# Power attention of a decoder: scores from single-pass products of split queries and keys, two heads at once

## What is computed

```python
q = (x @ Wq).reshape(B, T, 16, 128)          # 16 query heads
k = (x @ Wk).reshape(B, T, 8, 128)           # 8 key heads, each used by 2 query heads
v = (x @ Wv).reshape(B, T, 8, 128)
logG = cumsum(log_sigmoid(6.906768 + x @ Wg))
qk = einsum('bthd,bshd->bhts', q, k) / sqrt(128)
a  = where(causal, qk ** 2 * exp(logG[t] - logG[s]), 0)
y  = einsum('bhts,bshd->bthd', a, v) / (sum(a) + 1e-6)
out = y @ Wc + bc                            # then x + out and a layer norm
```

## Time and profile before

| what | value |
|---|---|
| median of 3 runs | 2582.27 us (2581.72 to 2593.28) |
| the profiled execution, its own time | 2584.34 us |
| its span, first to last instruction | 2582.6 us |
| TensorE busy | 2235.2 us, 87% of the span |
| VectorE, ScalarE, GpSimd busy | 1204.0, 981.8, 679.0 us |
| mean granted TensorE clock | 0.916 of full speed |
| chain that ended last, by engine | PE 22%, issue 6%, DVE 6%, ACT 4% |
| matmul line 330, high weights by high x | 384 matmuls of 512 columns, 397 ns each |

### The profile page before, as it was taken

The page is one execution under the profiler, slowest core; times in us unless marked ns, Lnnn a source line. Parts: engine busy times, 40 slices in busy tenths (PEclk is TensorE's granted clock), DMA queues, the critical chain, the costliest instruction groups (busy, mean ns, idle before and its releaser), DMA issues. The chain is left out here.

```text
span 2582.6 us, 38373 instructions
## 1 busy us (share of the span) xinstructions
PE 2235.2 (87%) x14368; PEld 1799.7 (70%) x14368; DVE 1204.0 (47%) x3113; ACT 981.8 (38%) x2234; POOL 679.0 (26%) x693
## 2 busy tenths in 40 slices
PE   5999999999998688878999999858898847888774
PEld 3989988988987466666888877656565436767542
DVE  2343333343335566655111113336777745677656
ACT  2222222222222466633121111223655635777632
POOL 2442332332231121112343410023443331332110
PEclk8999999999999767789999999887999868999886
DMA  5000000000000110010010000023332130000001
GB/s 191 1 29 13 9 29 13 9 21 13 9 1 1 64 44 26 1 54 33 25 50 17 17 1 1 1 49 53 51 54 49 28 114 13 14 26 10 1 9 65
DMA packets 34631, 78.08 MB, mean 30 GB/s; under 512 B 5264, under 2 KB 17680, under 8 KB 31504
## 3 DMA queue, kind: packets, MB, share of 16 engines
q1 hardware_dynamic: 34448, 75.63, 10.4%
HBM read 55.16 MB, written 4.19 MB: 23 GB/s over the span
## 5 line engine op out<-in xcount | busy, mean ns | idle before, releaser
L1108 PE MATMUL PS<-WH,bXH 128*128 128x512 f32 x512 | 200.9, 392 | 5.4 <-POOL WL L1385 5.4
L1108 PE MATMUL PS<-WL,bXH 128*128 128x512 f32 x512 | 200.4, 391 | 0.0
L1108 PE MATMUL PS<-WH,bXL 128*128 128x512 f32 x512 | 200.4, 391 | 0.0
L558 DVE TENSOR_TENSOR xN<-PS,xN 128x512 f32<-128x512 f32 x128 | 88.5, 691 | 228.0 <-PE PS L361 228.0
L1790 DVE TENSOR_REDUCE aM<-PS 128x4 f32<-128x1024 f32 x128 | 155.0, 1221 | 52.1 <-PE PS L1630 51.1
L1303 DVE SCALAR_TENSOR_TENSOR s<-s,cf,PS 128x256 f32<-128x256 f32 x112 | 53.8, 480 | 249.1 <-ACT s L1223 240.1
L1733 ACT ACTIVATE aPT<-PS 128x1024 f32<-128x1024 f32 x128 | 129.4, 1024 | 69.8 <-PE PS L1650 68.5
L1223 ACT ACTIVATE s<-PS 128x256 f32<-128x256 f32 x128 | 49.0, 383 | 277.3 <-PE PS L1108 277.3
L330 PE MATMUL PS<-aXH,QKH 128*128 128x512 f32 x384 | 152.3, 397 | 0.0
L643 POOL TENSOR_TENSOR E<-E,DM 128x256 f32<-128x256 f32 x64 | 47.1, 736 | 392.4 <-ACT E L475 392.4
L330 PE MATMUL PS<-aXH,QKL 128*128 128x512 f32 x384 | 149.6, 390 | 0.0
(11 more groups left out here) (405 smaller groups left out, 6264.1 us busy)
## 6 DMA issues: line engine op xcount, KB each, us to landing
sg<-in_gu SPq DMA_DIRECT2D x8, 1024.0 KB, 4.9
aqs<-aQH SPq DMA_DIRECT2D x64, 128.0 KB, 4.2
gQK<-in_Wqk SPq DMA_DIRECT2D x8, 768.0 KB, 4.2
V<-in_xT SPq DMA_DIRECT2D x4, 1024.0 KB, 6.3
gC<-in_Wc SPq DMA_DIRECT2D x8, 512.0 KB, 3.6
xN<-in_x SPq DMA_DIRECT2D x4, 1024.0 KB, 8.7
cst<-in_cT SPq DMA_DIRECT2D x8, 512.0 KB, 4.8
cV<-in_c SPq DMA_DIRECT2D x8, 512.0 KB, 4.0
```

The source lines that it names most:

```text
L558: e.tensor_tensor(xN[:, t, :], PS[:, b, :], xN[:, t, :], ALU.add).then_inc(o_add.sem, 1)
L1108: mm = e.matmul(PS[:, b, :], x[:, kc, 128 * t:128 * t + 128], w[:, kc, :], start=kc == 0 and i == 0, stop=kc == KC - 1 and i == 2)
```

## The change

The projected queries and keys are stored as two F32R tiles, `qkH` and `qkL`, in place of the float32 tile `qk`. ScalarE writes `qkH` for all three m (three copies a step instead of two); VectorE writes `qkL` as the difference of PSUM and `qkH` (three subtractions a step instead of one copy), and releases the PSUM room. The scores of both heads of a sequence are one product: three single-pass matmuls of 512 columns (2 heads by 256 queries, first 128 keys) into the first bank, and three of 256 columns (2 heads by 128 queries, last 128 keys) into the first half of the second bank. The square reads the 768 columns in one run; `sq` and `aT` have the new order of columns; the multiply into `aT` becomes two instructions, of 512 and 256 columns; the logits' copy before turn 0 becomes one instruction in place of two.

```diff
-        qk = W("qk", [128, 3, 512])
+        qkH, qkL = W("qkH", [128, 3, 512], F32R), W("qkL", [128, 3, 512], F32R)
...
-        sq = W("sq", [128, 2, 384])
-        aT = W("aT", [128, 2, 2, 384])
+        sq = W("sq", [128, 768])
+        aT = W("aT", [128, 2, 768])
...
-    qk_mm, q_out, k_out = K.flag("pe_qk", 3 * N), K.flag("act_q", 2 * N), K.flag("dve_q", N)
+    qk_mm, q_hi, q_lo = K.flag("pe_qk", 3 * N), K.flag("act_q_hi", 3 * N), K.flag("dve_q_lo", 3 * N)
...
             for m in range(3):
-                R.use(("qk", n, m), 1, k_out.upto(n + 1) if m == 1 else q_out.upto(2 * n + 1 + m // 2))
+                R.use(("qk", n, m), 1, q_lo.upto(3 * n + m + 1))
...
                 for h in (0, 1):
-                    e.matmul(PS[:, b, 130 * h:130 * h + 129], aT[:, j, h, 0:128], v0, start=True, stop=True,
+                    e.matmul(PS[:, b, 130 * h:130 * h + 129], aT[:, j, 256 * h:256 * h + 128], v0, start=True, stop=True,
                              skip_group_check=True)
...
                 if j == 0:
-                    e.wait_ge(*q_out.upto(2 * n + 2))
-                    e.wait_ge(*k_out.upto(n + 1))
-                for h in (0, 1):
-                    q0 = 256 * j
-                    e.matmul(PS[:, b + h, 0:256], qk[:, 2, q0:q0 + 128], qk[:, h, q0:q0 + 256], start=True, stop=True)
-                    mm = e.matmul(PS[:, b + h, 256:384], qk[:, 2, q0 + 128:q0 + 256], qk[:, h, q0 + 128:q0 + 256],
-                                  start=True, stop=True, skip_group_check=True)
+                    e.wait_ge(*q_hi.upto(3 * n + 3))
+                    e.wait_ge(*q_lo.upto(3 * n + 3))
+                q0 = 256 * j
+                for i, (k, q) in enumerate(pair3((qkH, qkH), (qkL, qkL))):
+                    e.matmul(PS[:, b, :], k[:, 2, q0:q0 + 128], q[:, 0:2, q0:q0 + 256], start=i == 0, stop=i == 2)
+                for i, (k, q) in enumerate(pair3((qkH, qkH), (qkL, qkL))):
+                    mm = e.matmul(PS[:, b + 1, 0:256], k[:, 2, q0 + 128:q0 + 256], q[:, 0:2, q0 + 128:q0 + 256],
+                                  start=i == 0, stop=i == 2)
                 mm.then_inc(s_mm.sem, 1)
...
-            for m in (0, 2):
+            for m in range(3):
                 b = rooms["qk", n, m][0]
                 if m == 0 and n:
                     e.wait_ge(*s_mm.upto(2 * n))
                 e.wait_ge(*qk_mm.upto(3 * n + m + 1))
-                e.activation(qk[:, m, :], PS[:, b, :], ACTF.Copy).then_inc(q_out.sem, 1)
+                e.activation(qkH[:, m, :], PS[:, b, :], ACTF.Copy).then_inc(q_hi.sem, 1)
...
-                    e.activation(sq[:, :, :], PS[:, b:b + 2, 0:384], ACTF.Square, scale=SC).then_inc(s_sq.sem, 1)
+                    e.activation(sq[:, :], PS[:, b:b + 2, :].rearrange("p a c -> p (a c)")[:, 0:768], ACTF.Square, scale=SC).then_inc(s_sq.sem, 1)
...
-            e.tensor_copy(aT[0:8, p % 2, 0, :], PS[0:8, b, 0:384])
-            e.tensor_copy(aT[0:8, p % 2, 1, 0:128], PS[0:8, b, 384:512]).then_inc(lg_out.sem, 1)
+            e.tensor_copy(aT[0:8, p % 2, 0:512], PS[0:8, b, :]).then_inc(lg_out.sem, 1)
...
                 if n:
                     e.wait_ge(*s_mm.upto(2 * n))
-                e.wait_ge(*qk_mm.upto(3 * n + 2))
-                e.tensor_copy(qk[:, 1, :], PS[:, rooms["qk", n, 1][0], :]).then_inc(k_out.sem, 1)
+                for m in range(3):
+                    e.wait_ge(*q_hi.upto(3 * n + m + 1))
+                    e.tensor_tensor(qkL[:, m, :], PS[:, rooms["qk", n, m][0], :], qkH[:, m, :].bitcast(F32),
+                                    ALU.subtract).then_inc(q_lo.sem, 1)
...
-                    e.tensor_tensor(aT[:, j, :, :], sq[:, :, :], E[:, j:j + 1, :].broadcast_to([128, 2, 384]),
-                                    ALU.mult).then_inc(s_at.sem, 1)
+                    for c, w, k in ((0, 512, 0), (512, 256, 256)):
+                        at = e.tensor_tensor(aT[:, j, c:c + w].rearrange("p (h q) -> p h q", h=2),
+                                             sq[:, c:c + w].rearrange("p (h q) -> p h q", h=2),
+                                             E[:, j:j + 1, k:k + w // 2].broadcast_to([128, 2, w // 2]), ALU.mult)
+                    at.then_inc(s_at.sem, 1)
```

More of the change, by code:

```diff
@@ L314, in tensor @@
             for i in range(4):
-                src = aT[0:8, p % 2, 0, 128 * i:128 * i + 128] if i < 3 else aT[0:8, p % 2, 1, 0:128]
+                src = aT[0:8, p % 2, 128 * i:128 * i + 128]
                 mm = e.transpose(PS[:, b, 32 * p + 8 * i:32 * p + 8 * i + 8], src, idF[0:8, 0:8])
@@ L377, in attend @@
                 for h in (0, 1):
-                    e.matmul(PS[:, b, 130 * h:130 * h + 129], aT[:, j, h, 0:128], v0, start=True, stop=True,
+                    e.matmul(PS[:, b, 130 * h:130 * h + 129], aT[:, j, 256 * h:256 * h + 128], v0, start=True, stop=True,
                              skip_group_check=True)
                 for h in (0, 1):
-                    e.matmul(PS[:, b + 1, 130 * h:130 * h + 129], aT[:, j, h, 128:256], v0, start=True, stop=False,
+                    e.matmul(PS[:, b + 1, 130 * h:130 * h + 129], aT[:, j, 256 * h + 128:256 * h + 256], v0, start=True, stop=False,
                              skip_group_check=True)
-                    mm = e.matmul(PS[:, b + 1, 130 * h:130 * h + 129], aT[:, j, h, 256:384], v1, start=False,
+                    mm = e.matmul(PS[:, b + 1, 130 * h:130 * h + 129], aT[:, j, 512 + 128 * h:640 + 128 * h], v1, start=False,
                                   stop=True, skip_group_check=True)
```

## The result

The changed kernel takes 2568.42 us (median of 14 runs, 2562.87 to 2579.85), the kernel before 2587.76 us (14 runs, 2576.10 to 2598.24; the 2582.27 us shown above were the median of the first three of them). The ratio is 0.9932 with a 95% interval of 0.9913 to 0.9951: 0.7% faster, some 18 us. The profiled execution of the changed kernel took 2577.13 us, with a span of 2575.4 us; it is one of its slower ones.

A forecast was written before the change was run, and what follows sets the result against it. TensorE's queue was taken to bound layer 0's self attention. Scores -16.2, split multiply +0.2 and logits copies -0.2 sum to -16.2 us, giving 2566 us against the median of 2582.27; range 2557 to 2576.

The forecast's parts named there:

- TensorE's queue is the time in turns 0 to 29: Layer 0's self attention: TensorE always busy, so one microsecond out of its queue is one microsecond of the kernel.
- 2.62 against 2.08 us: TensorE's time for one turn's scores, before and after the change; a gain of 0.54 us a turn.
- the upper bound: 512-column scores at 0.230 us: 0.007 us extra for each of 12 matmuls, 0.08 us a turn, 2.5 us in all.
- 30 turns count: Of 32 turns with scores, all but turns 30 and 31 give 0.54 us each, 16.2 us together.
- there the shorter scores only lengthen that wait: Turns 30 and 31: TensorE already waits 1.84 and 1.83 us for `yN`, so shorter scores gain nothing there.
- the 0.2 us forecast for the start: Before turn 0, four times two logits copies become one: -0.2 us in all, between 0 and -1.1.
- ScalarE and VectorE cost nothing: Each turn: ScalarE's extra 0.60 us copy and VectorE's three 0.68 us subtractions fit in idle time.
- 1.8: Microseconds to spare between VectorE's last subtraction of a turn and its first add of `out`.
- The split multiply: Multiply into `aT` as two instructions: 0.08 us for each j, hidden in normal turns, +0.2 us in turn 31.
- The gain is made and partly lost later: Rival: after 786 us low-clock stretches may shift; gain sinks to 8 us, 2574 us; chance 0.22.
- Weight loads that don't hide: Rival: 12 score weight loads a turn in the open, 1.3 us more a turn, 2605 us; chance 0.04.
- VectorE late at the transposes: Rival: VectorE over 0.9 us later at `attended`, TensorE waits, gain gone, 2582 us; chance 0.04.

The follow-up runs named there:

- fill_norm_turns: Changed kernel plus 8 overwritten TensorE matmuls in `turn`, meant ahead of the yN waits of turns 30 and 31; 2583.37 us, ratio 0.9953 to the kernel before.
- two and four products: Changed kernel without the low-keys-by-high-queries score product: 2546.1 us, ratio 0.9840; with low keys by low queries added: 2588.22 us, 1.0009 (to the kernel before).
- fill_scores: Changed kernel plus 8 overwritten TensorE matmuls ahead of the second sequence's score products in turns 30 and 31; 2578.73 us, ratio 0.9946 to the kernel before.

## Why the prediction was right

Forecast were 2566 us and 16.2 us of gain; measured were 2568.42 us, a ratio of 0.9932, and on three chips or sets of runs 0.9932, 0.9946 and 0.9916. That is the side and about the size. The nearness of the whole is partly luck. The self attention gave 13.7 us and not 16.2. The stages after cross0 gave 3.4 us that nobody forecast: from the first product with the experts' weights on, both profiles of the kernel before take 1453.1 and 1453.2 us, and eleven of the twelve profiles of the changed kernel and its variants 1449.3 to 1450.0 (`fill_norm_turns` has 1453.2). It lies in the attention stages of the second layer, whose code is the same; the cause is open. And the kernel before, from whose first three runs the 2566 us were counted, has a median 5.5 us higher over all 14. Step by step:

- **TensorE's queue is the time in turns 0 to 29**: shown. No wait of TensorE came up in normal turns, and the queue's slope is one to one between two and four products.
- **2.62 against 2.08 us**: the old side was right, the new one is 2.11, since the 512-column products come at 0.233 and not at 0.2267 us. I had named this pace as the upper bound, but tied it to the two runs of columns; with one run it is the same. The isolated-stream figure of the Trainium skill ("TensorE: Matmul & The Clock Gate", "Back-to-back issue gap") is 0.216 us for 512 columns. The trace does not agree: 0.227 to 0.233, each with a weight load of its own.
- **30 turns count**: right for the scores, since the waits of turns 30 and 31 grew from 1.84 to 2.36 us. But "there the shorter scores only lengthen that wait" was the step that failed: the longer wait let the clock fall, which cost 1.6 us. `fill_scores` takes the wait away and the 1.6 us come back. So 14.1 us reach the end of the stage in place of 16.2: 30 x 0.51 = 15.3 from the turns, 0.4 from the start, less 1.6 for the clock. The 0.4 is chance: the first score matmul starts at 80.1 us where it was 80.5, but at 79.2 and 81.9 in the other two profiles of the changed kernel, so the 0.2 us forecast for the start can't be seen either. From the first score matmul on the gain is 13.7 us, with the other two profiles 13.6 and 12.7.
- **ScalarE and VectorE cost nothing**: right as to waits. The high half of m = 2 is followed by VectorE's subtraction, from 340.67 us in turn 12, and the first add waits for TensorE until 343.27:

```profile
340.67 0.69 DVE L578 TENSOR_TENSOR qkL<-PS,qkH 128x512 fp32r<-128x512 f32 x1 [2.03 <-ACT qkH L470]
343.27 0.69 DVE L558 TENSOR_TENSOR xN<-PS,xN 128x512 f32<-128x512 f32 x1 [1.91 <-PE PS L361]
```

  1.91 us are left, for which I had said 1.8. Even 3.9 us more of work bring no wait, though the turn becomes 0.13 us longer for a reason that stays open.
- **The split multiply**: 1.03 us for two instructions in place of 0.96, 0.07 for each j (forecast 0.08). The 0.2 us that this was to cost at the stage's end are not seen: from the square of turn 31 to the last matmul of the stage there are 31.6 us in both kernels.
- **The rivals.** Weight loads that don't hide: no, 12 loads a turn are inside the paces. VectorE late at the transposes: no. "The gain is made and partly lost later" has a true core in turn 30. For cross0 nothing is shown: what it takes, 253 to 280 us over fourteen profiles, differs within one kernel (260.7 and 272.1 for the kernel before) and at one start. The medians leave little room for a loss there: they are 19 us apart, the self attention and the stages after cross0 give 17, and the interval (0.9913 to 0.9951) is 13 to 23 us.

## What to carry to other kernels

Where one engine is busy for all of a stage at its full clock, cost a change of its work by the distances between starts in its queue, and it comes out to a few per cent. Where that engine already waits, don't count a shorter piece of work as neutral: the wait becomes longer, and if the clock falls behind it the work that follows pays. A stage whose own time varies by more than the gain hides it in the sum; take the gain at the end of the stage that was changed, and ask the whole only for its sign.

## What the runs showed of the hardware that I had not expected

- At turn 30 a wait of TensorE of 1.84 us, and 0.50 more after two transposes, left the granted clock at 1.00 in both profiles of the kernel before; 2.36 us at the same place let it fall in all three profiles of the changed kernel (mean 0.65 to 0.66 between 780 and 785 us); 1.66 and 0.54 us left it at 1.00. It isn't sure at each such wait: behind the 2.36 us of turn 31 the transposes ran slowly in the third profile and at full pace in the first.
- Cross0 takes anything between 253.2 and 280.2 us, with a mean clock between 0.79 and 0.64 from 870 to 1100 us, in executions whose matmuls there are the same and in which it starts within 40 us (835.2 to 874.4). What sets it is open. Of the 13.0 us between the spans of the two profiles of the kernel before it is 11.4. Whether it makes the spread of the runs without a profile is not shown; their clock goes the same way (2562.87 us at a mean of 0.918, 2579.85 at 0.910).
- Single-pass matmuls of 512 columns come 0.2267 or 0.233 us apart in one kernel, in whole stretches, with nobody waiting. Making the moving operand one run did not change the 0.233 of the scores; `out` went from 0.227 to 0.232 in both kernels with more work for VectorE, whether the added tile had 24 or 128 bytes. What sets the pace is open.
